# Two layers of a transformer stage: the weighted values moved to the end of TensorE's step, the mask put into 64x64 tiles, the values' projections half a unit later

## The reference, cut to what matters

```python
h = shift_token(x); q, k, v = split(h @ wqkv)          # 3 x 512 columns
q = l2norm(q) * qs; k = l2norm(k) * ksc; q, k = rotary_xpos(q, k)
bk, bv = look_around(bk), look_around(bv)              # own block of 64 keys and the one before
sim = einsum('bhwid,bhwjd->bhwij', bq, bk)
mask = (i < j) | (i > j + WINDOW) | (j == -1)
attn = softmax(where(mask, -max, sim))
x = x + einsum('bhwij,bhwjd->bhwid', attn, bv) @ wo
h = layernorm(shift_token(x)) * lg + lb
a, g = split(h @ w1 + b1); x = x + (a * gelu(g)) @ w2 + b2
```

## Time and profile before

| | us |
|---|---|
| median of 3 runs | 1372.63 (1371.99 to 1372.76) |
| the profiled execution | 1375.34 |
| its span, first to last instruction | 1373.5 |
| VectorE's first maximum of stage F | 661.78 |
| VectorE's first maximum of unit 4 / 21 / 31 | 741.43 / 1093.59 / 1316.13 |

### The profile page before, as it was taken

The page is one execution under the profiler, slowest core; times in us unless marked ns, Lnnn a source line. Parts: engine busy times, 40 slices in busy tenths (PEclk is TensorE's granted clock), DMA queues, the critical chain, the costliest instruction groups (busy, mean ns, idle before and its releaser), DMA issues.

```text
span 1373.5 us, 37019 instructions
## 1 busy us (share of the span) xinstructions
PE 1234.7 (90%) x12288; PEld 966.9 (70%) x12288; DVE 1126.7 (82%) x2210; ACT 974.5 (71%) x1804; POOL 1068.3 (78%) x1431
## 2 busy tenths in 40 slices
PE   4599999999999999998679999999999999999985
PEld 3477777777777777777457777777777777777764
DVE  3589888888888888886688888888888988989873
ACT  4467667677676676665568788888888787878761
POOL 1866666666667666658799999999999999999961
PEclk9799999999999999999999999999999999999997
DMA  5000000000000000000111121111122112121110
GB/s 174 1 8 13 7 14 13 12 11 11 10 11 11 8 8 10 9 9 15 43 40 44 43 49 46 41 47 46 43 52 52 46 45 52 41 51 47 44 36 24
DMA packets 87053, 44.15 MB, mean 32 GB/s; under 512 B 43908, under 2 KB 80176, under 8 KB 86960
## 3 DMA queue, kind: packets, MB, share of 16 engines
q1 hardware_dynamic: 86960, 42.95, 12.2%
HBM read 19.86 MB, written 6.29 MB: 19 GB/s over the span
## 4 chain that ended last, share of the span: by engine, by line
POOL 39%; PE 24%; issue 22%; DVE 8%; ACT 3%; SPq 2%; POOLq 1%; DMA 0%; DVEq 0%; ACTq 0%
POOL rnorm L716 9%; POOL probs L668 7%; POOL kT L705 7%; POOL probs L766 4%; POOL kT L719 3%; PE bank L1453 2%; PE bank L1373 2%; PE bank L1432 2%; PE bank L1414 2%; PE bank L1488 2%; PE bank L1334 2%; PE bank L1347 2%; PE bank L1307 1%; PE bank L1502 1%; SPq L479 1%
## 5 line engine op out<-in xcount | busy, mean ns | idle before, releaser
L668 POOL TENSOR_TENSOR probs<-probs,coef 128x1024 f32<-128x1024 f32 x128 | 242.0, 1902 | 5.0
L716 POOL TENSOR_TENSOR rnorm<-norm,halves 128x8 f32<-128x8 f32 x128 | 213.7, 1669 | 10.7
L1078 DVE TENSOR_REDUCE mx<-bank 128x8 f32<-128x512 f32 x256 | 160.2, 668 | 33.5 <-PE bank L1347 33.5
L845 ACT ACTIVATE wT<-bank 128x512 f32<-128x512 f32 x256 | 138.2, 595 | 60.4 <-PE bank L1334 60.2
L1053 DVE TENSOR_REDUCE sums<-probs 128x16 f32<-128x1024 f32 x128 | 152.1, 1211 | 27.3 <-ACT probs L860 27.3
L860 ACT ACTIVATE probs<-probs 128x1024 f32<-128x1024 f32 x128 | 135.5, 1058 | 50.4 <-DVE probs L1086 50.0
L705 POOL TENSOR_TENSOR kT<-qT 128x512 f32<-128x512 f32 x128 | 163.7, 1279 | 6.9 <-DVE qT L1127 6.9
L1086 DVE TENSOR_TENSOR probs<-bank,mx 128x512 f32<-128x512 f32 x256 | 163.0, 678 | 0.3
L1347 PE MATMUL bank<-kT,qT 64*128 64x256 f32 x1024 | 147.2, 406 | 17.1 <-DVE probs L1086 17.1
L1373 PE MATMUL bank<-wT,v 128*64 128x128 f32 x2048 | 140.1, 279 | 24.4 <-ACT qT L816 11.4
L1373 PEld LDWEIGHTS bank<-wT,v 128*64 128x64 f32 x2048 | 109.5, 136 | 61.3 <-ACT wT L845 27.8
(11 more groups left out here) (130 smaller groups left out, 3126.4 us busy)
## 6 DMA issues: line engine op xcount, KB each, us to landing
probs<-f_v SPq DMA_DIRECT2D x96, 128.0 KB, 2.3
res<-stage_x SPq DMA_DIRECT2D x48, 128.0 KB, 3.7
xn<-in_x SPq DMA_DIRECT2D x16, 128.0 KB, 2.1
xr<-in_x SPq DMA_DIRECT2D x16, 128.0 KB, 2.1
stage_x<-xo SPq DMA_DIRECT2D x32, 64.0 KB, 1.6
hn<-stage_x SPq DMA_DIRECT2D x32, 64.0 KB
mn<-mid SPq DMA_DIRECT2D x64, 32.0 KB
stage_x<-yo SPq DMA_DIRECT2D x16, 128.0 KB, 2.1
```

What stands on the lines that cost most here:

```text
L668: nc.gpsimd.tensor_tensor(out=e[:, :, :, :], in0=e[:, :, :, :], in1=coef[r][:, 2, A_REP * ng:A_REP * (ng + 1), :].unsqueeze(3).broadcast_t ...
L716: nc.gpsimd.tensor_tensor(out=rnorm[:, at], in0=norm2[:, 1, at], in1=halves[:, 0:F_HEADS], op=ALU.pow).then_inc(rnorm_set, 1)
L845: nc.scalar.activation(wT[hp][:, :, :, :], banks[4 + hp][:, :], ACT.Copy).then_inc(wT_read, 1)
L1078: ins = nc.vector.tensor_reduce(m[:, 2 * k:2 * k + 2, :], both[k][:, :].rearrange("p (h c k) -> p h c k", h=2, c=CHUNKS), AX.X, ALU.max)
```

## The change

- `weighted_values` moves from between the two `qkT` fills to the last place of TensorE's step, behind `down`, directly ahead of the next step's mask.
- The mask is no longer two matmuls of 128 rows by 128 output partitions with 512 columns, but four of 64 by 64 with 512 columns, in the same tile shape as the scores. The host's mask and the buffer keep their size (the two halves now are "first block" and "all others", and the quarter is chosen by block). Between the waits of `scores` and its first matmul stands a new `pe.sem_inc(scores_waited, 1)`.
- ScalarE's copy `foT` moves from between its two `qkT` copies to the head of the next step. `output` still is two steps behind.
- `v` of tile 1 of a unit is projected and read in that unit's own even step, `v` of tile 0 of the next unit in the odd step. Before, both were done one unit ahead in the even and odd step. The count stays one per step. SyncE's shifts follow: the one with one DMA now comes at the even step's end, the one with two at the odd step's end.
- One `v` leaves the prologue.

```diff
-F_ATT_LAG, F_XO_LAG = 1, 2
+F_ATT_LAG, F_PV_LAG, F_XO_LAG = 1, 2, 2
...
-    0: ["mT", ("qk", 4, 0, 1), ("qk", 4, 1, 1), ("v", 2, 0, 1)],
-    1: [("hT", 1, 0, 2), ("qk", 4, 2, 1), ("qk", 4, 3, 1), ("v", 2, 1, 1)],
+    0: ["mT", ("qk", 4, 0, 1), ("qk", 4, 1, 1), ("v", 2, 1, 0)],
+    1: [("hT", 1, 0, 2), ("qk", 4, 2, 1), ("qk", 4, 3, 1), ("v", 2, 0, 1)],
...
@@ ScalarE, body
+                        if f_exists(turn, s, F_PV_LAG):
+                            act.wait_ge(f_o_made, n - F_PV_LAG + 1)
+                            wait(act, f_made["out"], n - F_PV_LAG - 1)
+                            nc.scalar.activation(foT[(s - F_PV_LAG) % 2][:, :, :], banks[4][:, :].rearrange("p (m q) -> p m q", m=INNER // P),
+                                                 ACT.Copy).then_inc(f_o_read, 1)
...
-                        if f_exists(turn, s, F_ATT_LAG):
-                            act.wait_ge(f_o_made, late + 1)
-                            wait(act, f_made["out"], late - 1)
-                            nc.scalar.activation(foT[(s - F_ATT_LAG) % 2][:, :, :], banks[4][:, :].rearrange("p (m q) -> p m q", m=INNER // P),
-                                                 ACT.Copy).then_inc(f_o_read, 1)
                         if prepares(turn, p, tile):
                             transposed(unit + tile, 4 * (p + tile) + 3 - 2 * tile, 3 - 2 * tile, turn)
-                        if prepares(turn, p):
-                            values_read(unit + 1, TILES * (p + 1) + tile, tile, turn)
+                        if prepares(turn, p, tile):
+                            values_read(unit + tile, TILES * (p + tile) + 1 - tile, 1 - tile, turn)
...
@@ TensorE, scores
-                    for k in range(2):
-                        nc.tensor.matmul(banks[k][:, :].rearrange("p (a k) -> p a k", a=4), ident16[:, :],
-                                         mask[:, tile, :].unsqueeze(1).broadcast_to([P, 4, F_KEYS]), start=True, stop=False)
+                    pe.sem_inc(scores_waited, 1)
+                    for w in range(2):
+                        for k in range(2):
+                            lo = F_HD * k
+                            nc.tensor.matmul(banks[k][WINDOW * w:WINDOW * (w + 1), :].rearrange("p (a k) -> p a k", a=4),
+                                             ident16[lo:lo + WINDOW, lo:lo + WINDOW],
+                                             mask[lo:lo + WINDOW, int(tile + w > 0), :].unsqueeze(1).broadcast_to([WINDOW, 4, F_KEYS]),
+                                             start=True, stop=False)
...
@@ TensorE, body
-                        if follows:
-                            weighted_values(it, late, late_s // TILES, late_s % TILES)
                         following("values")
...
-                        if prepares(turn, p):
-                            ahead("v", TILES * (p + 1) + tile)
+                        if prepares(turn, p, tile):
+                            ahead("v", TILES * (p + tile) + 1 - tile)
                         following("gates")
                         following("mix")
                         following("down")
+                        if follows:
+                            weighted_values(it, late, late_s // TILES, late_s % TILES)
```

More of the change, by code:

```diff
@@ L143 @@
 F_PREPARED = {
-    0: ["mT", ("qk", 4, 0, 1), ("qk", 4, 1, 1), ("v", 2, 0, 1)],
-    1: [("hT", 1, 0, 2), ("qk", 4, 2, 1), ("qk", 4, 3, 1), ("v", 2, 1, 1)],
+    0: ["mT", ("qk", 4, 0, 1), ("qk", 4, 1, 1), ("v", 2, 1, 0)],
+    1: [("hT", 1, 0, 2), ("qk", 4, 2, 1), ("qk", 4, 3, 1), ("v", 2, 0, 1)],
 }
-F_PRE = [("hT", 0), ("qk", 0), ("qk", 1), ("qk", 2), ("qk", 3), ("v", 0), ("v", 1), ("qkT", 0), ("qkT", 1), ("hT", 1)]
+F_PRE = [("hT", 0), ("qk", 0), ("qk", 1), ("qk", 2), ("qk", 3), ("v", 0), ("qkT", 0), ("qkT", 1), ("hT", 1)]
 F_PER = {"hT": 1, "qk": 4, "v": 2, "qkT": 4}
@@ L242, in build @@
         table = [sb(f"table{l}", [P, TILES, 4, F_HD]) for l in range(LAYERS)]
-        mask = sb("mask", [P, TILES, F_KEYS], BF16)
+        mask = sb("mask", [P, 2, F_KEYS], BF16)
         ident16 = sb("ident16", [P, P], BF16)
@@ L331, in build @@
         vs_in = [sem(f"vs{p}_in") for p in range(PAIR)]
-        pads_set = sem("pads_set")
+        pads_set, scores_waited = sem("pads_set"), sem("scores_waited")
         m_bn, m_stats, m_eps, m_rstd, hc_set, mid_kept, resb_set = (
@@ L539, in pre @@
                     sp.wait_ge(pads_set, N_PADS)
-                    for tile in range(TILES):
-                        sp.wait_ge(f_read["v"], tile + 1)
-                        shift_values(0, 0, tile)
+                    sp.wait_ge(f_read["v"], 1)
+                    shift_values(0, 0, 0)
                 def body(it, turn, layer_of):
@@ L569, in body @@
                             sp.dma_start(results[layer][:, bass.ds(b, 1), :, :], yo[four][:, :, :]).then_inc(m_out[four], 16)
-                        if prepares(turn, p):
-                            wait(sp, f_read["v"], TILES * c + 3)
-                            shift_values(c + 1, (p + 1) % PAIR, 0)
+                        if prepares(turn, p, 0):
+                            wait(sp, f_read["v"], TILES * c + 2)
+                            shift_values(c, p, 1)
                         if f_exists(turn, TILES * p + 1, F_XO_LAG):
@@ L580, in body @@
                         if prepares(turn, p):
-                            wait(sp, f_read["v"], TILES * c + 4)
-                            shift_values(c + 1, (p + 1) % PAIR, 1)
+                            wait(sp, f_read["v"], TILES * c + 3)
+                            shift_values(c + 1, (p + 1) % PAIR, 0)
                         if f_exists(turn, TILES * p + 1, F_LATE["z"]) and layer_of(p - 4) == LAYERS - 1:
@@ L1472, in pre @@
                     pe.wait_ge(read["out"], BATCH * TILES)
-                    for kind in ("v", "qkT", "hT"):
-                        pe.wait_ge(f_read[kind], 2)
+                    for kind, count in (("v", 1), ("qkT", 2), ("hT", 2)):
+                        pe.wait_ge(f_read[kind], count)
                 def scores(unit, n, p, tile):
@@ L1602, in score_mask @@
     within = (key >= q % WINDOW) & (key <= q % WINDOW + WINDOW)
-    first = within & ((q >= WINDOW) | (key >= WINDOW))
+    first = within & (key >= WINDOW)
     return np.where(np.concatenate([first, within], axis=1), 0.0, MASKED).astype(np.float32)
```

## The result

| | before | after |
|---|---|---|
| median of the runs | 1372.70 us (4 runs, 1371.99 to 1375.02) | 1400.33 us (4 runs, 1398.00 to 1402.69) |
| ratio after / before | | 1.020, 95% interval 1.0185 to 1.0215 |
| profiled execution | 1375.34 us (span 1373.5) | 1402.69 us (span 1400.9) |

What follows compares the result with a forecast made beforehand. Bound: a TensorE-ScalarE-VectorE loop as long as GpSimd's queue in the first layer, GpSimd in the second. 17 units +25.9, filling +1.5, ten last units 0, drain +1.2: +28.6 us, so 1401; 8-in-10 range 1387 to 1415.

Steps and rivals of the forecast that it cites:

- The loop: First layer: a loop through TensorE, ScalarE and VectorE closes in 20.64 us, like GpSimd's queue; added work lengthens it to 22.24.
- The weighted values' regained gap: Between bank 5's fills: removing 1.23 us regains only 0.28 in even steps, as the second fill waits for ScalarE's copy.
- The weighted values ahead of the mask, +1.23 a step: TensorE's step end: weighted values enter the loop in both steps, adding 1.23 us to each.
- The mask: Ahead of the scores: four 64x64 tiles run abreast in 0.24 us instead of 0.53, gaining 0.29 per step; semaphore free.
- foT at zero: ScalarE: moving the foT copy to the next step's head costs nothing; bound 0.59 us in one step of two.
- v and the DMAs at zero: Projection v half a unit later and SyncE's DMAs moved with it: no cost.
- The second layer at zero: Last ten units: GpSimd's queue takes 22.25 us each, the new loop of 22.24 just fits under it; cost 0.
- The drain, 1.2: Program end: one set of weighted values behind down and ahead of the last outputs, 1.2 us (bounds 0 and 2.5).
- A: Rival: GpSimd sets the pace with 20.64 us units and covers the change; time stays 1372.6 us; chance 7%.
- B: Rival: masks don't run four abreast; 1417 us two at a time, 1446 one after another; chance 9%.
- C: Rival: faster, cheaper masks gain 0.29 per step and the weighted values merely rotate TensorE's step; 1362.8 us; chance 4%.
- D: Rival: VectorE and ScalarE reorder their waits and absorb half the price; 1387 us; chance 7%.

Runs made afterwards that it cites:

- e1: Changed kernel with the weighted values back between the two bank-5 fills in even steps, last only in odd steps: 1392.15 us, ratio 1.0137.
- e2: Changed kernel with the weighted values back between the two bank-5 fills in odd steps, last only in even steps: 1378.30 us, ratio 1.0034.
- e3: Changed kernel with the old two full mask matmuls and no extra semaphore instruction: 1415.06 us, ratio 1.0309.
- e9: Changed kernel with ScalarE normalising 4 pieces of the probabilities instead of 3, GpSimd the rest: 1394.32 us, ratio 1.0156.
- e11: As e1, but with the even step's foT copy put back between ScalarE's two earlier copies: 1381.37 us, ratio 1.0063.
- e6: Kernel before with only v half a unit later, its DMAs and waits moved along: 1372.25 us, ratio 1.0001.
- e5: Kernel before with only the mask changed to four 64x64 tiles, plus the semaphore instruction: 1373.85 us, ratio 1.0005.
- e7: Kernel before with ScalarE normalising 4 pieces of the probabilities instead of 3, GpSimd the rest: 1365.75 us, ratio 0.9949.
- e8: Kernel before with both the four 64x64 masks and ScalarE normalising 4 pieces instead of 3: 1360.27 us, ratio 0.9909.
- e12: As e8, but with the floor of the norms (128x8) moved from GpSimd to VectorE: 1402.78 us, ratio 1.0211.

## Why the prediction was right, and where it was off

- **The loop, and that every piece in it costs its full length.** Right, and shown: the unit grew to 22.05 with GpSimd waiting, e1 and e2 give the two steps' parts, e3 the masks', e9 leaves the first layer where it was. The forecast unit was 22.24; the terms that make the difference follow.
- **The weighted values' regained gap.** Forecast: the second fill starts 911.55 - 911.27 = 0.28 earlier behind the first one. Measured: it starts 923.72 - 922.29 = 1.43 behind it, where it was 1.64, so 0.21 is regained. The handover was taken as 0.06 and is 0.13 (copy to 922.99 + 0.60 = 923.59, fill at 923.72). By the prediction's way of counting, from 922.29 + 0.41, the stand is 1.02 against 0.95; the 0.82 of the row counts from the modelled end of the fill. In the odd step the row has 0.94, forecast "about 0.9".
- **The weighted values ahead of the mask, +1.23 a step.** Slightly too large: from down's start to the mask's it is 2.62 - 1.44 = 1.18. That is 1.08 for themselves (938.60 to 939.68) and 0.10 for the way into their tiles of 128x64 (down takes 1.54 to its neighbour's start, before 1.44). The way out costs the same to either mask: in e3, with the full one, it is also 1.08.
- **The mask.** 0.24 forecast, 0.24 seen; with the scores' 0.06 it is worth 0.35 a step (e3) instead of 0.29. The semaphore's instruction shows no cost. In the odd step the two terms, 0.05 and 0.06, make 11.87 of 11.97; in the even step, where the gap took 0.07 of it back, and the piece from the scores to the first fill is 0.05 shorter, 10.19 of 10.27. Together 22.05 of 22.24, and 17 units of it the 3.3 us by which the first layer came out lower.
- **foT at zero.** Right for after's first layer, but not because the copy is free: e1, without the even step's delay, pays 0.3 us a unit for it, and e11 takes that away again.
- **v and the DMAs at zero.** Right (e6).
- **The second layer at zero.** Off by 1.1 us. GpSimd still waits for no one there (no such row between 1117 and 1340), so the term's reason holds; but its own work grew. L715 takes 1.80 us instead of 1.67 when it meets VectorE's hc, which the new phase brings about once a unit, 9 of 40 times in units 21 to 30; its mean is 1697 ns against 1666 before. 9 x 0.13 = 1.2 us is about the whole difference. e2 has 8 such cases and the same unit of 22.40, e1 and e11 have none and a unit of 22.26. GpSimd's and VectorE's timelines of the kernel after:

```profile
1220.25 0.59 DVE L1144 TENSOR_SCALAR hc<-mn,mmv,mrstd 128x128 f32<-128x128 f32 x2
1220.31 1.80 POOL L715 TENSOR_TENSOR rnorm<-norm,halves 128x8 f32<-128x8 f32 x1
```

- **The drain, 1.2.** It can't be judged. In the last 54 to 60 us TensorE's granted clock changes between its two levels, and how long it is at the lower one differs from kernel to kernel and from run to run. e9, with nearly the same work behind the last maximum as after (one piece of the probabilities more is divided on ScalarE), is 5.5 us shorter there, at a granted clock of 0.95 against 0.82; its 303 matmul records are busy for 33.45 us, after's 303 for 38.89 (the stretch is e9's, from its last maximum to its end):

```profile
1338.62:1393.10 54.48, 33.45 (x303) 27.08 (x302) 26.88 (x81) 21.98 (x41) 15.87 (x26) 0.95 0.11 30
```

  After's own four runs fall in two pairs, 1402.7 and 1402.2 at a clock of 0.979, 1398.5 and 1398.0 at 0.986, and the median of 1400.33 lies between them. Before's profiled execution lies 2.7 us above its median as after's lies 2.4 above its own, so most of this falls out of the 27.35. The forecast's nearness, 1.2 us by the profiled executions and 0.7 by the medians, is better than its terms, and that is luck: the 17 units were overestimated by 3.3, the second layer and the two ends underestimated by 2.7 together, and the stretch ahead of stage F, which the change doesn't touch, was 0.6 shorter.
- **The rivals.** A, GpSimd covers it: refuted by the waits of the page after and by e9. B: refuted by the row of the masks and by e3. C: the cheaper masks exist (the 0.7 of e3), but in e5 they bring nothing behind GpSimd's queue, and with the fills side by side and the values ahead of the mask the loop gets longer. D, half the price absorbed: 17 units show 22.6 of 25.9, so no. Over before's 20.7 e1 costs 0.77 a unit and e2 0.25, together less than the 1.35 of after, but this is no absorption: the masks' gain of 0.70 is in each of them, so twice in the sum. The loop with the new masks alone is about 20.59 - 0.70 = 19.9 us, an estimate from e7 and e3 that no run shows, since GpSimd's queue holds e8 at 20.20. Counted from it e11 costs 1.3 and e2 1.1, together 2.4, and after 2.2: from the loop's own length the prices add to within about 0.2 us.

## What to carry to other kernels

Look for loops across engines beside the fullest engine: sum one unit from an event to the same event a unit later, and if the sum is the unit, everything put into it costs its full length, whatever the occupancies say. Two limits of equal length have to be shortened together (a unit of the first layer: e5 0, e7 0.05 to 0.1, both 0.44), while the loop lengthened shows at once. (Of e7's 7 us about half, 10 x 0.37, lies in the second layer, where GpSimd alone is the limit.) An operation that seems idle filler between two uses of one buffer may be what hides the copy-out: before moving it, ask what then fills that time.

## What the runs showed of the hardware

- VectorE and GpSimd keep each other from running at certain pairs of operations, for the length of a whole instruction. VectorE's TENSOR_SCALAR on 128x8 takes 0.17 us clear of it and 0.73 to 1.02 beside GpSimd's product of 128x512, ending with it (51 cases in e12's units 4 to 20, ends 0.03 us apart); GpSimd's TENSOR_SCALAR on 128x8 0.24 alone and up to 0.53 beside hc. The Trainium skill (SBUF — State Buffer, Who interferes with whom) says that the two engines share a pair of ports as an exclusive lock, held for the whole instruction, and that `tensor_scalar` of VectorE can take it in its 2-port mode; these rows agree. Not every pair does: 17 times in the same units VectorE's 128x8 runs inside GpSimd's power on 128x2 (L740 of e12, 0.69 us) and takes 0.17 all the same, and L715 beside hc (after) loses only 0.13. The page also says that TensorE and ScalarE never wait for it; no run here contradicts this. A duration read where the other engine was quiet can therefore be far too short for another place (e12), and a change of phase alone can cost 0.1 us a unit (the second layer after).
- Matmuls in four 64x64 tiles run beside each other in bf16 as in f32: four of 512 columns in 0.24 us, two full ones of 512 columns with their change of shape in 0.53.
- Going from full 128x128 work into the weighted values' 128x64 tiles costs TensorE about 0.1 us, an estimate from starts: down takes 1.54 to its neighbour's start after and 1.44 before, a fill 0.53 ahead of the values and 0.41 ahead of a projection. Going on from them costs the same into four 64x64 masks (after) and into a full mask (e3): 1.08 from their start to the mask's in both. No run measured a change by itself.
- TensorE's clock in the thin end of the program is at either of its levels, 1.2 or 2.4 GHz (in after the 5 us from 1360 have a granted clock of 0.50, those from 1370 1.00), and how long it is at each differs from run to run: the granted clock over the last stretch was 0.82 (after), 0.84 (before), 0.92 (e1) and 0.95 (e9, e11), with TensorE busy for 33 to 39 of 54 to 60 us. That is 4 to 5 us on a kernel of 1400, more than several of the edits tried here.
